# Embedding interactions on one core: ten one-hot tables instead of eight, groups of 256 samples, and the layers two groups later

## The chip, the cores and the metric

One Trainium2 core runs the whole program. The metric is device time in microseconds, the median of several timed executions of one kernel. One further execution is profiled, and all rows below come from it.

## The reference

2048 samples have 128 dense features and 26 ids, one for each table. A sample's 27 vectors of 128 numbers are its dense features and its 26 table rows. All 351 products of two of them go, with the dense features (twice), through three layers.

```python
e = jnp.stack([tbl_0[ids[:, 0]], ..., tbl_25[ids[:, 25]]], axis=1)
combined = jnp.concatenate([dense_features[:, None, :], e], axis=1)       # 2048 x 27 x 128
interactions = jnp.einsum('bnd,bmd->bnm', combined, combined)
z = jnp.concatenate([dense_features, interactions[:, _TRIU_I, _TRIU_J]], axis=1)
h = jnp.concatenate([z, r_dense_features], axis=1)                        # 607 columns
h = jnp.maximum(h @ W_top1 + b_top1, 0.0)                                 # 512
h = jnp.maximum(h @ W_top2 + b_top2, 0.0)                                 # 256
y = h @ W_top3
```

Twelve tables (8 to 11, 15 to 19, 23 to 25) have 1000 rows; the others have 1250 to 125000.

## The kernel before

**Two ways to a table row.** Eight 1000-row tables (`LOOKED`) are kept in SBUF, split into a high and a low part, whose products are added. A *look* (`look`, L333) multiplies them with a 0/1 matrix `match` that the vector engine makes by comparing the samples' ids with row numbers (`matches`, L465): 16 matmuls of 256 samples each, and the result already has features along the partitions. The other 18 tables are *gathered* (`gather_tile`, L294): GpSimd issues one indirect DMA for each table and tile of 128 samples, 288 in all, and TensorE transposes what lands (`turn`, L319), in groups of four tables.

**Stages of a tile.** `turned` holds the 27 vectors of each sample. `gram` (L354) multiplies them with themselves, 27x27, one small matmul a sample. The result is copied out (L451), written by SP to a DRAM scratch and read back along the diagonals (`repack`), so that `pairs` holds 3 chunks of 117 products by 128 samples. Then `layer1` (L365, L368), `layer2` (L379) and `layer3` (L386) run on 128 samples.

**Order.** All orders are written out by hand; the engines meet by semaphores. One iteration of the loop over `m` does two tiles, that is 256 samples: 8 looks, 9 groups of turns (36 transposes), 4 gram steps and two sets of layers. The layers stand one tile behind the grams. `rows` has two buffers of 18 tables, so a tile's first gather waits until the tile two before has been turned. There is one PSUM bank for looks; ACT copies six of the eight to `looked_sb` (L564) and puts all of them in place later (`unpack`, L576).

**Start.** SP loads the eight tables of 500 KB, 125 rows each, one after another (L255). ACT rounds each to its high part (L554), DVE takes the difference (L473). ACT does all eight before it copies the first look out (L564).

Of the kernel before, what the change touches and what calls it, by code (L numbers as in the profile page):

```python
# [9 lines left out]
SLOT = 28  # L30
LOOKED = [8, 9, 10, 11, 15, 16, 17, 18]
GATHERED = [k for k in range(TABLES) if k not in LOOKED]
LOOKS = len(LOOKED)
HALF = LOOKS // 2
EARLY = 2
STAGED = LOOKS - 2
PARTS = 8
GROUP_OF = 4
GROUPS = -(-len(GATHERED) // GROUP_OF)
STEPS = 2  # L40
AT_LAYER = [1, 2, 3]
IN_QUADRANT = P // STEPS // 4
SHIFTS = (FEATURES - 1) // 2
WRAPS = FEATURES - SHIFTS
CHUNK_I = 9
CHUNKS = FEATURES // CHUNK_I
CHUNK_ROWS = CHUNK_I * SHIFTS
BANK = 512
# [6 lines left out]
def tables_of(group):  # L55
    return GATHERED[group * GROUP_OF:(group + 1) * GROUP_OF]


def runs_of(some_tables):

    runs = []
    for n, k in enumerate(some_tables):
        if runs and runs[-1][1] + runs[-1][2] == k:
            runs[-1][2] += 1
        else:
            runs.append([n, k, 1])
    return runs


def looks_after(m, u, group):  # L70

    looks = [(m + 1, r) for r in range(HALF)] if u else [(m, r) for r in range(HALF, LOOKS)]
    if isinstance(m, int) and m + u == 0:
        looks = [(0, r) for r in range(EARLY, LOOKS)]
        return [look for n, look in enumerate(looks) if n * GROUPS // len(looks) == group]
    return [look for n, look in enumerate(looks) if n * (GROUPS - 1) // len(looks) == group]


def build(nc, dense_t, index_rows, look_ids_rows, tables, w1_dense, w1_pairs, b1, w2, b2, w3, y):
    fp32, fp32r, int32 = mybir.dt.float32, mybir.dt.float32r, mybir.dt.int32
# [3 lines left out]
    tiles = batch // P  # L86
    assert batch % (2 * P) == 0 and tiles >= 6
    look_rows = tables[LOOKED[0]].shape[0] // PARTS

    assert all(tables[k].shape[0] == look_rows * PARTS for k in LOOKED)  # L90
    assert look_rows <= P and look_rows * PARTS <= 4096 and 2 <= LOOKS <= 8 and LOOKS % 2 == 0
    assert FEATURES < 32 and batch <= FEATURES * P

    ctx = ExitStack()
    with ctx:
# [9 lines left out]

        rows = [sbuf(f"rows{u}", [P, len(GATHERED), D]) for u in range(2)]
        index = sbuf("index", [P, tiles, TABLES], int32)
        turned = sbuf("turned", [D, 2, P, SLOT])
        grams = [sbuf(f"grams{u}", [P, FEATURES, P]) for u in range(2)]
        pairs = [sbuf(f"pairs{u}", [P, CHUNKS, P]) for u in range(2)]  # L110
        hidden1 = sbuf("hidden1", [P, L1, P])
        hidden2 = sbuf("hidden2", [P, L2, P])
        y_row = grams[0][32:33].rearrange("p a b -> p (a b)")[:, 0:batch]
        dense_sb = sbuf("dense_sb", [D, batch])
        identity = sbuf("identity", [P, P])


        look_ids = sbuf("look_ids", [P, LOOKS, 2 * P], int32)
        row_number = sbuf("row_number", [P, PARTS], int32)
        table_high = sbuf("table_high", [P, LOOKS, PARTS, D], fp32r)  # L120
        table_low = sbuf("table_low", [P, LOOKS, PARTS, D], fp32r)
        looked_sb = sbuf("looked_sb", [D, STAGED, 2 * P])
        match = [sbuf(f"match{b}", [P, PARTS, 2 * P], fp32r) for b in range(2)]
        w1_dense_two = sbuf("w1_dense_two", [D, 2, H1])
        w1_dense_sum = w1_dense_two[:, 0, :]
        w1_pairs_sb = sbuf("w1_pairs_sb", [CHUNK_ROWS, CHUNKS, H1])
# [4 lines left out]

        scratch = [nc.dram_tensor(f"scratch{u}", (FEATURES, FEATURES + SHIFTS, P), fp32).ap() for u in range(2)]

        def raw_table(n):


            place = turned[0:look_rows, 1] if n < 2 else grams[(n - 2) // 3][0:look_rows]
            at = (n if n < 2 else (n - 2) % 3) * PARTS * D
            return place.rearrange("p a b -> p (a b)")[:, at:at + PARTS * D]

        turn_ps = [psum(f"turn_ps{b}", [P, BANK]) for b in range(2)]
        gram_ps = [psum(f"gram_ps{b}", [P, BANK]) for b in range(2)]
        layer1_ps = [psum(f"layer1_ps{h}", [P, L1 // 2, P]) for h in range(2)]
        layer2_ps = layer1_ps[0]
        layer3_ps = layer1_ps[1][0:1, 0, :]
        row_number_ps = psum("row_number_ps", [P, PARTS])
        look_ps = psum("look_ps", [P, BANK])

        index_in = sem("index_in")
        look_ids_in = [sem(f"look_ids_in{h}") for h in range(2)]
        raw_table_in = [sem(f"raw_table_in{n}") for n in range(LOOKS)]
        dense_in = sem("dense_in")
        weights_in = sem("weights_in")

        gathered = [[sem(f"gathered{u}_{g}") for g in range(GROUPS)] for u in range(2)]
        tiles_opened = sem("tiles_opened")
# [3 lines left out]
        row_numbers_copied = sem("row_numbers_copied")  # L162
        tables_high = sem("tables_high")
        tables_split = sem("tables_split")
        weights_summed = sem("weights_summed")
        turn_done = [sem(f"turn_done{u}") for u in range(2)]
        turned_dve = sem("turned_dve")
        turned_act = sem("turned_act")
# [3 lines left out]
        unpacked = sem("unpacked")  # L172
        gram_done = sem("gram_done")
        grams_dve = sem("grams_dve")
        grams_act = sem("grams_act")
        scratch_in = [sem(f"scratch_in{u}") for u in range(2)]
        wraps_in = [sem(f"wraps_in{u}") for u in range(2)]
        pairs_in = [sem(f"pairs_in{u}") for u in range(2)]
# [6 lines left out]
        y_stored = sem("y_stored")  # L185

        READS = CHUNKS * 16

        def after(eng, sem, count):

            if not isinstance(count, int) or count > 0:
                eng.wait_ge(sem, count)

        def bank_of(u, group):

            return (GROUPS * u + group) % 2

        def groups_in_bank(bank, m, u, group):

            return GROUPS * m + (GROUPS * u + group + 1 - bank) // 2  # L200

        def next_look(m, r):
            return (m, r + 1) if r + 1 < LOOKS else (m + 1, 0)

        def has_next(m, r):
            return not (isinstance(m, int) and (m, r) == (tiles // 2 - 1, LOOKS - 1))

        block = ctx.enter_context(nc.Block())

        @block.sync  # L210
        def _(sp):
            def known(value):

                return value if isinstance(value, int) else sp.snap(sp.to_reg(value))

            def load_look_ids(m, h):

                row, matched = (known(v) for v in (2 * m + h, LOOKS * (m - 1) + HALF * (h + 1)))

                after(sp, match_ready, matched)  # L220
                sp.dma_start(look_ids[:, HALF * h:HALF * (h + 1), :].rearrange("p n s -> p (n s)"),
                             look_ids_rows[bass.ds(row, 1)].broadcast_to([P, HALF * 2 * P])).then_inc(
                                 look_ids_in[h], 16)
# [56 lines left out]
            for u in range(2):  # L280
                repack(last_m, u)
# [381 lines left out]
```

## Time and profile before

| | us |
|---|---|
| median of 3 runs (411.86 to 413.2) | 412.48 |
| profiled execution | 414.85 |
| its span, from the first to the last instruction | 413.0 |
| busy: PE / GpSimd / DVE / ACT | 329.0 / 275.3 / 231.0 / 142.9 |
| mean granted TensorE clock, of full speed | 0.971 |

The busy time of GpSimd leaves out what it needs between two DMA issues, so it understates how full that engine is. Busy PE contains matmuls whose starts lie closer together than they are long: prices are read from start to start.

### The profile page before, as it was taken

To read this page: it belongs to the slowest core of one execution; us is meant where nothing else is said; L and a number is where in the kernel's file an instruction comes from. 1 tells how busy PE (TensorE), PEld (TensorE's weight loads), DVE (VectorE), ACT (ScalarE), POOL (GpSimd) and SP (SyncE) were. 2 spreads that over 40 slices of the span, in tenths; PEclk is the share of its full clock that TensorE was granted. 3 is DMA by queue.
4 is the path that set the end of the run, shared out by engine and by line. 5 is a ranking of instruction groups with operands and counts; after the bars stand their busy time and mean duration, and the time that the engine had idled before them with its cause. 6 is when DMAs were issued, how large, how long until landed. Compare 5 with 4: busy or idle time off the path is not lost.

```text
span 413.0 us, 14244 instructions
## 1 busy us (share of the span) xinstructions
PE 329.0 (80%) x6240; PEld 303.9 (74%) x6240; DVE 231.0 (56%) x234; ACT 142.9 (35%) x305; POOL 275.3 (67%) x295
## 2 busy tenths in 40 slices
PE   0300487999999999999989897989898895977676
PEld 0300486989898989897979796979888895966675
DVE  2244288686758676866666656576476656332211
ACT  1222216326333633363336231553236332442211
POOL 5777704777777777777777777777777777776000
PEclk9999998999999999999999998999999998998889
DMA  6444662254443434352424333342525142324020
GB/s 182 156 160 164 214 197 75 68 154 111 116 108 109 117 104 116 98 144 77 133 82 122 99 105 112 94 125 63 156 65 152 51 118 53 99 71 109 15 64 1
DMA packets 20763, 44.99 MB, mean 109 GB/s; under 512 B 6198, under 2 KB 11942, under 8 KB 20179
## 3 DMA queue, kind: packets, MB, share of 16 engines
q1 hardware_dynamic: 11524, 25.76, 20.3%
q0 software_dynamic: 9216, 18.89, 17.2%
q8 instruction: 18, 0.29, 0.3%
q14 instruction: 5, 0.04, 0.0%
HBM read 37.27 MB, written 7.36 MB: 108 GB/s over the span
## 4 chain that ended last, share of the span: by engine, by line
POOL 39%; PE 27%; issue 14%; DMA 7%; SPq 5%; ACT 4%; DVE 3%; POOLq 0%; ACTq 0%
POOL rows L294 39%; PE look_ps L333 11%; DMA grams<-in_table 6%; SPq L255 4%; PE gram_ps L354 4%; PE layer_ps L368 4%; PE layer_ps L379 3%; PE turn_ps L319 3%; ACT turned L576 2%; PE layer_ps L365 2%; DVE match L465 2%; DVE grams L451 1%; PE layer_ps L386 1%; DMA rows<-in_table,index 1%; ACT hidden L548 0%
## 5 line engine op out<-in xcount | busy, mean ns | idle before, releaser
L294 POOL DMA_INDIRECT rows<-in_table,index x288 | 274.5, 953 | 104.9 <-issue 86.5
L333 PE MATMUL look_ps<-match,table_high 125*128 125x256 f32 x512 | 137.9, 305 | 50.2 <-ACT looked_sb L564 27.7
L465 DVE TENSOR_TENSOR match<-look_ids,row_number_ps 125x2048 fp32r<-125x2048 int32 x64 | 145.8, 2280 | 6.5 <-DMA look_ids<-in_look_ids_rows 4.3
L333 PEld LDWEIGHTS look_ps<-match,table_high 125*128 125x128 f32 x512 | 103.2, 202 | 54.0 <-issue 52.4
L333 PE MATMUL look_ps<-match,table_low 125*128 125x256 f32 x512 | 132.2, 293 | 0.0
L333 PEld LDWEIGHTS look_ps<-match,table_low 125*128 125x128 f32 x512 | 103.8, 203 | 0.0
L451 DVE COPY grams<-gram_ps 27x432 f32<-27x432 f32 x64 | 38.2, 597 | 51.3 <-PE gram_ps L354 50.8
L319 PE MATMUL turn_ps<-identity,rows 128*128 128x128 f32 x288 | 47.2, 287 | 21.4 <-DMA rows<-in_table,index 21.3
L354 PE MATMUL gram_ps<-turned 128*27 128x27 f32 x4096 | 54.0, 194 | 5.1 <-issue 1.9
L354 PEld LDWEIGHTS gram_ps<-turned 128*27 128x27 f32 x4096 | 44.8, 105 | 15.4 <-issue 8.7
L368 PE MATMUL layer_ps<-pairs,w_pairs_sb 117*128 117x128 f32 x384 | 55.4, 282 | 0.0
L319 PEld LDWEIGHTS turn_ps<-identity,rows 128*128 128x128 f32 x288 | 33.0, 144 | 27.3 <-issue 21.1
L451 ACT COPY grams<-gram_ps 27x432 f32<-27x432 f32 x64 | 32.8, 512 | 58.1 <-PE gram_ps L354 57.7
L438 DVE COPY turned<-turn_ps 128x512 f32<-128x512 f32 (+3 forms) x48 | 27.8, 594 | 42.1 <-PE turn_ps L319 41.4
L368 PEld LDWEIGHTS layer_ps<-pairs,w_pairs_sb 117*128 117x128 f32 x384 | 50.1, 199 | 0.0
L564 ACT COPY looked_sb<-look_ps 128x256 f32<-128x256 f32 x48 | 17.9, 372 | 92.7 <-PE look_ps L333 92.7
L481 DVE TENSOR_SCALAR hidden<-layer_ps,b_sb 128x128 f32<-128x128 f32 x32 | 9.8, 347 | 44.6 <-PE layer_ps L379 42.5
L548 ACT ACTIVATE hidden<-layer_ps,b_sb 128x128 f32<-128x128 f32 x64 | 20.0, 364 | 42.0 <-PE layer_ps L368 42.0
L379 PE MATMUL layer_ps<-hidden,w_sb 128*128 128x128 f32 x256 | 32.9, 284 | 1.4 <-ACT hidden L548 1.4
L438 ACT COPY turned<-turn_ps 128x512 f32<-128x512 f32 (+3 forms) x48 | 27.1, 584 | 19.5 <-PE turn_ps L319 19.3
L379 PEld LDWEIGHTS layer_ps<-hidden,w_sb 128*128 128x128 f32 x256 | 31.6, 201 | 1.8 <-ACT hidden L548 1.8
L365 PE MATMUL layer_ps<-dense_sb,w_dense_two 128*128 (+1 forms) x128 | 27.3, 295 | 2.3 <-DVE grams L488 1.8
(21 smaller groups left out, 101.8 us busy)
## 6 DMA issues: line engine op xcount, KB each, us to landing
look_ids<-in_look_ids_rows SPq DMA_DIRECT2D x16, 512.0 KB, 4.2
scratch<-grams SPq DMA_DIRECT2D x16, 364.5 KB
rows<-in_table,index POOLq DMA_INDIRECT x288
grams<-in_table SPq DMA_DIRECT2D x6, 500.0 KB
pairs<-scratch SPq DMA_DIRECT2D x48, 58.5 KB
scratch<-grams SPq DMA_DIRECT2D x16, 84.5 KB
dense_sb<-in_dense_t SPq DMA_DIRECT2D x1, 1024.0 KB, 5.0
turned<-in_table SPq DMA_DIRECT2D x2, 500.0 KB
```

Source lines behind the costliest of these rows:

```text
L294: pool.indirect_dma_start(out=rows[u][:, group * GROUP_OF + n, :], out_offset=None, in_=tables[k], in_offset=bass.IndirectOffsetOnAxis(ap= ...
L319: last = nc.tensor.transpose(turn_ps[bank][:, n * P:(n + 1) * P], rows[u][:, group * GROUP_OF + n, :], identity[:])
L333: last = nc.tensor.matmul(look_ps[:, 0:2 * P], part[0:look_rows, r, c, :], match[r % 2][0:look_rows, c, :], start=(c == 0 and part is tabl ...
L354: last = nc.tensor.matmul(gram_ps[step][s * 32:s * 32 + FEATURES, x * FEATURES:(x + 1) * FEATURES], of_sample, of_sample, start=True, stop ...
L365: nc.tensor.matmul(layer1_ps[o // 2][:, o % 2, :], w1_dense_sum[:, o * P:(o + 1) * P], dense_sb[:, bass.ts(2 * m + u, P)], start=True, sto ...
L368: last = nc.tensor.matmul(layer1_ps[o // 2][:, o % 2, :], w1_pairs_sb[:, c, o * P:(o + 1) * P], pairs[u][0:CHUNK_ROWS, c, :], start=False, ...
L379: last = nc.tensor.matmul(layer2_ps[:, o, :], w2_sb[:, c, o * P:(o + 1) * P], hidden1[:, c, :], start=(c == 0), stop=(c == L1 - 1))
L438: last = copy(turned[:, u, :, 1 + k:1 + k + length], bank[:, n * P:(n + length) * P].rearrange("d (f s) -> d s f", f=length))
L451: last = copy(grams[u][0:FEATURES, :, sample:sample + IN_QUADRANT], gram_ps[step][s * 32:s * 32 + FEATURES, 0:IN_QUADRANT * FEATURES].rear ...
L465: nc.vector.tensor_tensor(match[r % 2][0:look_rows], look_ids[0:look_rows, r].unsqueeze(1).broadcast_to(shape), row_number_ps[0:look_rows] ...
L548: last = nc.scalar.activation(hidden1[:, o, :], layer1_ps[o // 2][:, o % 2, :], ACT.Relu, bias=b1_sb[:, o:o + 1])
L564: nc.scalar.copy(looked_sb[:, r, :], look_ps[:, 0:2 * P]).then_inc(looked, 1)
```

## The change

- **Tables.** Ten tables are looked up, 16 gathered. The tenth looked table (23) is gathered for groups 0 to 3 (`EXTRA`, two more indirect DMAs and one more turn for each of these groups) and looked up from group 4 on.
- **Groups.** Everything works on groups of 256 samples: a group has 10 looks (9 in groups 0 to 3), 8 turns of four tables, 4 gram steps of 64 samples, one set of layers of 256 columns. Weights of the gram matmuls are 32 columns wide (five are not used).
- **Looks ahead.** Six looks of the next group are made while this group's last gathers land. PSUM has two banks for looks of two each, three for turns and grams (`mid_ps`), two for layers. ACT does every copy out of PSUM, DVE only matches and splits. `unpack` is gone: looks go straight to `turned`, of which there are two.
- **Layers.** The layers of group g-2 stand among the grams of g-1 and the turns of g.
- **Start.** Tables go through three raw buffers, each loaded as 112 and 13 rows; splits and looks of groups 0 and 1 are interleaved table by table.
- **Repack.** `grams` has 128 partitions; the scratch gets 864 and 416 KB a group, the read back is 12 DMAs of 117 rows of 256 bytes (before: 3 of 117 rows of 512 bytes a tile). In the last group the three chunks are issued by SP, ACT and GpSimd. `rows` is freed four tables at a time.
- The scratch that holds the software DMA's descriptors is set to 4096 bytes; ids for the looks are int16.

```diff
-LOOKED = [8, 9, 10, 11, 15, 16, 17, 18]
+LOOKED = [8, 9, 10, 11, 15, 16, 17, 18, 19, 23]
...
+EXTRA = (0, 1, 2, 3)
...
+N = 256
...
+        def load_pairs(eng, g, c, signal):
+            for s in range(QUADS):
...
+                eng.dma_start(pairs[0:CHUNK_ROWS, g % 2, c, s * IN_QUAD:(s + 1) * IN_QUAD], skewed).then_inc(signal, 16)
...
+            def load_raw(r):
...
+                after(sp, tables_split, r - RAWS + 1)
+                sp.dma_start(raw[b][0:SPREAD], rows_of[0:SPREAD]).then_inc(raw_in[b], 16)
+                sp.dma_start(raw[b][SPREAD:table_rows], rows_of[SPREAD:table_rows]).then_inc(raw_in[b], 16)
...
+            def repack(g):
+                sp.wait_ge(mid_out, gram_number(g, STEPS - 1) + 1)
...
+                sp.dma_start(flat[:, 0:FEATURES], grams[:]).then_inc(scratch_in, 16)
+                sp.dma_start(flat[:, FEATURES:WIDTH], grams[:, 0:SHIFTS]).then_inc(scratch_in, 16)
+                sp.wait_ge(scratch_in, SCRATCH_DMAS * (g + 1))
...
+                for c in range(CHUNKS if g + 1 < groups else 1):
+                    load_pairs(sp, g, c, pairs_in)
```

TensorE's new loop (the whole of it; `range` of g is 1 to 6):

```diff
+            for g in range(1, groups - 1):
...
+                gram(g - 1, 0)
+                turn(g, 0)
+                look(g, 6)
+                if g >= 2:
+                    layer1(g - 2, 0)
+                    layer1(g - 2, 1)
+                gram(g - 1, 1)
+                turn(g, 1)
+                look(g, 7)
+                if g >= 2:
+                    layer1(g - 2, 2)
+                    layer1(g - 2, 3)
+                gram(g - 1, 2)
+                turn(g, 2)
+                look(g, 8)
+                if g >= 2:
+                    layer2(g - 2)
+                gram(g - 1, 3)
+                turn(g, 3)
+                if g in EXTRA:
+                    turn_extra(g)
+                else:
+                    look(g, 9)
+                if g >= 2:
+                    layer3(g - 2)
+                turn(g, 4)
+                look(g + 1, 0)
+                look(g + 1, 1)
+                turn(g, 5)
+                look(g + 1, 2)
+                turn(g, 6)
+                look(g + 1, 3)
+                turn(g, 7)
+                look(g + 1, 4)
+                look(g + 1, 5)
```

**GpSimd's gathers.** The queue from its first gather on, before (288 gathers, a wait for each 18):

```order
L303 IOTA row_number 128x8
L294 DMA rows<-in_table,index 128x128 [waits index_in]
L294 DMA rows<-in_table,index 128x128 x35
L294 DMA rows<-in_table,index 128x128 [waits turn_done0]
L294 DMA rows<-in_table,index 128x128 x17
```

and after the change (`extra` is the tenth table's buffer; `turn_done` frees four tables of `rows`):

```order
L311 AFFINE_SELECT identity<-identity 128x128 [waits zeroed]
L322 DMA rows<-in_table,index 128x128 [waits first_index_in]
L322 DMA rows<-in_table,index 128x128 x15
L333 DMA extra<-in_table,index 128x128 [waits index_in]
L333 DMA extra<-in_table,index 128x128
L322 DMA rows<-in_table,index 128x128 [waits index_in]
L322 DMA rows<-in_table,index 128x128 x15
L322 DMA rows<-in_table,index 128x128 [waits turn_done]
L322 DMA rows<-in_table,index 128x128 x3
```

The queue is 264 gathers long instead of 288, and the waits stand before each four gathers; the two of `extra` come behind the first tile of groups 0 to 3.

**ACT's start.** Its queue from the last three of the eight table splits (`table_high`) on, before:

```order
L554 CAST table_high<-grams 125x1024 [waits raw_table_in5]
L554 CAST table_high<-grams 125x1024 [waits raw_table_in6]
L554 CAST table_high<-grams 125x1024 [waits raw_table_in7]
L564 COPY looked_sb<-look_ps 128x256 [waits look_done] x2
L564 COPY looked_sb<-look_ps 128x256 [waits look_done,tables_split,dense_in]
L564 COPY looked_sb<-look_ps 128x256 [waits look_done]
L438 COPY turned<-turn_ps 128x128x4 [waits turn_done0]
L564 COPY looked_sb<-look_ps 128x256 [waits look_done] x2
```

and after, from the first split on:

```order
L554 CAST table_high<-grams 125x1024 [waits raw_in0]
L554 CAST table_high<-pairs 125x1024 [waits raw_in1]
L554 CAST table_high<-hidden 125x1024 [waits raw_in2]
L554 CAST table_high<-grams 125x1024 [waits raw_in0]
L561 COPY turned<-look_ps 128x256x2 [waits look_done] x2
L554 CAST table_high<-pairs 125x1024 [waits raw_in1]
L572 COPY turned<-mid_ps 128x128x4 [waits turn_done]
L554 CAST table_high<-hidden 125x1024 [waits raw_in2]
L572 COPY turned<-mid_ps 128x128x4 [waits turn_done]
L561 COPY turned<-look_ps 128x256x2 [waits look_done] x2
```

The first copy of a look stood behind eight splits and stands behind four; the others alternate with splits and turns.

**TensorE's end.** Behind the last turns, before (the grams are those of the last tile):

```order
L354 MATMUL gram_ps<-turned 27x27 [waits looked,grams_dve,unpacked,grams_act,turned_act,turned_dve]
L354 MATMUL gram_ps<-turned 27x27 x63
L354 MATMUL gram_ps<-turned 27x27 [waits grams_act,grams_dve]
L354 MATMUL gram_ps<-turned 27x27 x63
L386 MATMUL layer_ps<-hidden,w_sb 1x128 [waits hidden2_ready]
L386 MATMUL layer_ps<-hidden,w_sb 1x128
L365 MATMUL layer_ps<-dense_sb,w_dense_two 128x128 [waits y_copied,pairs_in0]
L368 MATMUL layer_ps<-pairs,w_pairs_sb 128x128 x3
```

and after, from the last turn on:

```order
L364 MATMUL mid_ps<-identity,rows 128x128 [waits gathered1_3,mid_out]
L364 MATMUL mid_ps<-identity,rows 128x128 x3
L405 MATMUL layer_ps<-dense,w_dense_sum 128x256
L408 MATMUL layer_ps<-pairs,w_pairs_sb 128x256 x3
L390 MATMUL mid_ps<-turned 32x27 [waits mid_out]
L390 MATMUL mid_ps<-turned 32x27 x63
L417 MATMUL layer_ps<-hidden,w_sb 128x256 [waits hidden1_ready]
L417 MATMUL layer_ps<-hidden,w_sb 128x256 x7
L390 MATMUL mid_ps<-turned 32x27 [waits mid_out]
L390 MATMUL mid_ps<-turned 32x27 x63
L424 MATMUL layer_ps<-hidden,w_sb 1x256 [waits hidden2_ready]
L424 MATMUL layer_ps<-hidden,w_sb 1x256
```

Before, one layer 2, two gram steps and a layer 3 stood between the last turn and the last two layer sets (128 samples each); now a quarter of a layer 1, two gram steps, a layer 2 and a layer 3 of 256 samples stand there, and two layer sets of 256 samples follow.

## Rows read from the trace of the kernel before

**Rows 1.** The head of the page.

```profile
span 413.0 us, 14244 instructions
```

**Rows 2.** Windows: length, busy us (instructions) of each engine, clock, DMA share, GB/s.

```profile
103.76:143.74 39.98, 39.15 (x780) 36.40 (x781) 27.57 (x29) 16.67 (x38) 30.23 (x33) 1.00 0.41 113
...
166.52:380.00 213.48, 190.61 (x3809) 175.88 (x3806) 125.38 (x132) 81.55 (x181) 161.37 (x171) 0.97 0.36 100
```

**Rows 3.** Timeline of GpSimd: start, us, instruction [idle before, releaser].

```profile
4.22 1.10 POOL L294 DMA_INDIRECT rows<-in_table,index  x1 [2.65 <-DMA index<-in_index_rows]
...
66.66 0.94 POOL L294 DMA_INDIRECT rows<-in_table,index  x1 [15.08 <-PE turn_ps L319]
...
126.58 0.94 POOL L294 DMA_INDIRECT rows<-in_table,index  x1 [0.30 <-PE turn_ps L319]
```

**Rows 4.** The chain that ended last, at the last gather: start, us, what.

```profile
380.00 2.79 DMA rows<-in_table,index
```

**Rows 5.** Timeline of TensorE: the first matmul of the first two looks.

```profile
15.93 0.55 PE L333 MATMUL look_ps<-match,table_high 125*128 125x256 f32 x1 [15.93 <-DVE table_low L473]
...
47.42 0.56 PE L333 MATMUL look_ps<-match,table_high 125*128 125x256 f32 x1 [27.74 <-ACT looked_sb L564]
```

**Rows 6.** Timeline of ACT: the first look is copied out.

```profile
46.91 0.36 ACT L564 COPY looked_sb<-look_ps 128x256 f32<-128x256 f32 x1
```

**Rows 7.** Timeline of DVE: the first match.

```profile
6.04 2.29 DVE L465 TENSOR_TENSOR match<-look_ids,row_number_ps 125x2048 fp32r<-125x2048 int32 x1 [4.26 <-DMA look_ids<-in_look_ids_rows]
```

**Rows 8.** Groups by line: count, busy us, mean ns, idle before.

```profile
L465 DVE TENSOR_TENSOR match<-look_ids,row_number_ps 125x2048 fp32r<-125x2048 int32 x64 | 145.8, 2280 | 6.5 <-DMA look_ids<-in_look_ids_rows 4.3 <-PE look_ps L333 1.7
...
L354 PEld LDWEIGHTS gram_ps<-turned 128*27 128x27 f32 x4096 | 44.8, 105 | 15.4 <-issue 8.7 <-DVE turned L438 0.3
...
L438 ACT COPY turned<-turn_ps 128x512 f32<-128x512 f32 x24 | 17.6, 733 | 12.8 <-PE turn_ps L319 12.6
...
L473 DVE TENSOR_TENSOR table_low<-grams,table_high 125x1024 fp32r<-125x1024 f32 x6 | 7.4, 1226 | 15.5 <-ACT table_high L554 15.5
```

**Rows 9.** Timeline of TensorE around 200 to 221 us.

```profile
199.70 0.60 PE L319 MATMUL turn_ps<-identity,rows 128*128 128x128 f32 x4
200.06 0.36 PE L333 MATMUL look_ps<-match,table_high 125*128 125x256 f32 x1
...
202.06 1.95 PE L379 MATMUL layer_ps<-hidden,w_sb 128*128 128x128 f32 x16
203.85 0.60 PE L319 MATMUL turn_ps<-identity,rows 128*128 128x128 f32 x4
...
211.37 1.81 PE L354 MATMUL gram_ps<-turned 128*27 128x27 f32 x128
213.11 0.66 PE L319 MATMUL turn_ps<-identity,rows 128*128 128x128 f32 x4
...
217.52 0.48 PE L365 MATMUL layer_ps<-dense_sb,w_dense_two 128*128 x2
...
221.19 0.60 PE L319 MATMUL turn_ps<-identity,rows 128*128 128x128 f32 x4
```

**Rows 10.** Timeline of all engines at the end of the span.

```profile
383.32 3.43 PE L379 MATMUL layer_ps<-hidden,w_sb 128*128 128x128 f32 x16
...
392.57 0.28 SPq L234 DMA_DIRECT2D scratch<-grams  x1
...
396.44 2.34 SPq L249 DMA_DIRECT2D pairs<-scratch  x3
...
399.15 2.05 PE L379 MATMUL layer_ps<-hidden,w_sb 128*128 128x128 f32 x16 [0.71 <-ACT hidden L548]
...
401.90 0.60 PE L386 MATMUL layer_ps<-hidden,w_sb 128*1 128x128 f32 x4 [0.70 <-DVE hidden L481]
...
411.19 0.24 SPq L283 DMA_DIRECT2D out_y<-grams  x1
```

**Rows 11.** DMA issues: KB each, median us to landing.

```profile
dense_sb<-in_dense_t SPq DMA_DIRECT2D x1, 1024.0 KB, 5.0
```

More of the change, by code:

```diff
@@ L52, with build @@
 L2 = H2 // P
[L55 to L82, printed above, removed]
+def build(nc, dense_t, index_t, look_rows_t, tables, w1_dense, w1_pairs, b1, w2, b2, w3, y):
+    fp32, fp32r, int32, int16 = mybir.dt.float32, mybir.dt.float32r, mybir.dt.int32, mybir.dt.int16
     ALU = mybir.AluOpType
@@ L198, in groups_in_bank, with looks_of, look_order @@
[L198 to L206, printed above, removed]
-        block = ctx.enter_context(nc.Block())
+        def looks_of(g):
+            return LOOKS - 1 if g in EXTRA else LOOKS
+        def look_order():
+            yield from ((g, r) for r in range(AHEAD) for g in (0, 1))
+            yield from ((g, r) for g in (0, 1) for r in range(AHEAD, looks_of(g)))
+            yield from ((g, r) for g in range(2, groups) for r in range(looks_of(g)))
@@ L310, in _ @@
+            pool.wait_ge(scratch_in, SCRATCH_DMAS * groups)
+            pool.wait_ge(layer1_done, 2 * (groups - 2))
+            load_pairs(pool, groups - 1, CHUNKS - 1, last_chunk_in)
         @block.tensor
         def _(pe):
[L312 to L321 removed]
@@ L388, in layer3 @@
                 last.then_inc(layer3_done, 1)
-            def tile(m, u, grams=True, layers=True, looks=True, last=False):
-                gm = m - 1 + u
-                for group in range(GROUPS):
-                    turn(m, u, group)
-                    if looks:
-                        for look_of in looks_after(m, u, group):
-                            look(*look_of)
-                    if grams and group < STEPS:
-                        gram(gm, 1 - u, group)
-                    if layers and group == AT_LAYER[0]:
-                        layer1(m - 1, u)
-                    if layers and group == AT_LAYER[1] and not last:
-                        layer2(m - 1, u)
-                    if layers and group == AT_LAYER[2] and not last:
-                        layer3(m - 1, u)
@@ new lines, in _ @@
+            g = groups - 1
+            for k in range(STEPS):
+                gram(g - 1, k)
+                turn(g, k)
+                look(g, AHEAD + k)
+            layer1(g - 2, 0)
+            layer1(g - 2, 1)
+            gram(g, 0)
+            layer1(g - 2, 2)
+            gram(g, 1)
+            turn(g, 4)
+            turn(g, 5)
+            turn(g, 6)
+            turn(g, 7)
+            layer1(g - 2, 3)
+            gram(g, 2)
+            layer2(g - 2)
+            gram(g, 3)
+            layer3(g - 2)
```

801 lines of the change are left out of this document (451 added, 350 removed).

## The prediction, made blind

> **What bounds the kernel now.** I read the windows first: they show two regimes. In one whole iteration, from 103.76 to 143.74 us, TensorE is busy 39.15 of 39.98 us at clock 1.00; from 166.52 to 380.00 us it is busy 190.6 of 213.5 us [rows 2]. GpSimd's busy time hides that it is the full engine there: in its timeline the gathers stand 0.30 us apart, 0.94 us each; the first starts at 4.22 us, and one waited for long, 15.08 us, for a turn [rows 3]. The last, the 288th, starts at 380.00 us [rows 4]. So a gather takes (380.00 - 4.22 - 15.08) / 287 = 1.257 us, and an iteration's 36 take 45.2 us, against TensorE's 39.98 us. The chain that ended last passes through that last gather, which has landed 2.79 us after its start, at 382.79 us; the end is 413.0 us [rows 1], a tail of 30.2 us.
>
> The start decides where GpSimd first waits. TensorE's first look is at 15.93 us, its second at 47.42 us [rows 5], because ACT copies the first one out only at 46.91 us, behind its eighth split [rows 6]. Till then the `rows` buffers fill, and GpSimd stands.
>
> So the time is: 4.22 us, 288 gathers, the 15.08 us stall, and the tail.
>
> **GpSimd's term.** 16 x 16 + 4 x 2 = 264 gathers, 24 fewer. The wait before each four instead of before each eighteen adds nothing: a gather whose wait for a turn is fulfilled starts after the same 0.30 us as any other, as at 126.58 us [rows 3]. The stall goes if four rows are turned in time. The last gather then starts at 4.22 + 263 x 1.257 = 334.8 us and has landed at 337.6 us, 45.2 us earlier. By the same grid the last gathers of groups 1, 2, 3 and 4 (the 68th, 102nd, 136th and 168th) have landed at 91.2, 134.0, 176.7 and 216.9 us.
>
> **The start.** For each of the first six tables DVE makes two matches of 2.28 us and a split of 1.23 us [rows 8], 5.8 us; for each of the next three 3.5 us. From about 6 us, where its first match is now [rows 7], that ends at 6 + 34.8 + 10.5 = 51 us. Loading a table has to keep this pace: dense features of 1024 KB land in 5.0 us [rows 11], and 500 KB cannot be slower than DVE's 5.8 us unless they come as before, in about 4.5 us ((47.42 - 15.93) / 7), which would do too. I take 56 us for the end of the start, with a few us of half clock. Turns 0 to 4 stand among these looks, so the first `rows` buffer is free well before GpSimd comes to it again at 4.2 + 34 x 1.257 = 47 us.
>
> In group 1, which has no layers, TensorE has work for 28 us (4 x 1.74 + 8.5 x 0.36 + 9 x 2.00, by the prices below) and then waits for the gathers: its last turn stands at 91.2 us. Behind it stand two looks. So a start that ends anywhere before about 65 us costs nothing.
>
> **TensorE's term.** From start to start: a turn 0.36, a look 2.00, a layer 2 of 128 columns 1.79, a gram step 1.74, a layer 1 of 128 columns 3.67 us [rows 9]; a layer 3 0.60 us [rows 10]. Eight looks, nine turns, four grams and two layer sets add to 38.3 us; the iteration took 39.98 us, so 1.7 us go into handing over. I start from the 39.98 us:
> - two looks more, +4.0 us (one look and half a turn more in groups 2 and 3, +2.2 us); one turn fewer, -0.36 us.
> - Layers of 256 columns are not in the trace. Above, they cost as much as two of 128 columns. Below, each of a matmul's two passes costs what a look's single pass over 256 columns costs (2.00 / 16 = 0.125 us), which would halve a layer set. I take the upper end: same number type, same columns, so 12.1 us a group and no change.
> - Gram weights of 32 columns instead of 27: the same 1.74 us below, 32/27 of it (2.06 us) above. I take the lower end, since what streams is still 27 columns.
> - Copies out, matches: ACT's copy of a turn is 0.73 us, DVE's match 2.28 us [rows 8], so ten matches are 23 us of a group and lie beside TensorE. Work queued behind a late copy is TensorE's third next step, since three banks rotate.
>
> So a group takes 41.8 us (2 and 3) and 43.6 us (4 to 6) on TensorE, against GpSimd's 42.7 and 40.2 us. Group 2 starts at 91.2 + 0.4 + 4.0 = 95.6 us. Group 2 is done at 138.4 us (134.0 and what stands behind its last turn), group 3 at 181.1 us (176.7 + 4.4), group 4 at 181.1 + 43.6 = 224.7, group 5 at 268.3, group 6 at 311.9 us: from group 4 on TensorE is the slower of the two, slightly. Group 7 up to its second four turns has 4 x (1.74 + 0.36 + 2.00), three quarters of a layer 1 (5.5) and two grams (3.5), 25.4 us: 337.3 us. The last gather has landed at 337.6 us. The two meet; the turns are done at 338.8 us.
>
> **The tail.** A quarter of a layer 1 (1.84), gram (1.74), layer 2 (3.58), gram (1.74), layer 3 (1.2), to 348.9 us. Layer 1 of group 6 (7.34), 1.0 us for its last two activations (0.71 us for two of half the size [rows 10]), layer 2 (3.58), 0.95, layer 3 (1.2): 363.0 us. The same again for group 7: 377.0 us. Copy and store: 0.4, then 1.8 us as now (411.19 us to the end [rows 1, 10]). Span 379.2 us.
>
> Beside it runs group 7's repack. From the last gram's copy (348.3 us) the scratch write of 1280 KB lies between the 3.9 us of today's 449 KB (392.57 to 396.44 us [rows 10]) and that times 2.85, 11 us; nearest is the load of 1024 KB in 5.0 us [rows 11], so 6.2 us. Twelve read backs at 0.78 us [rows 10], split over three queues, land by about 362 us, 1 us before layer 1 wants them. With 11 us it is 3 us late, and the end with it.
>
> **Sum.** 413.0 - 45.2 (24 gathers and the stall) + 1.2 (turns end behind the landing) + 10.2 (tail 40.4 instead of 30.2) = 379.2 us. The profiled execution lies 1.85 us above its span and 2.37 us above the median, so the median should be 378.7 us.
>
> **Weighing a rule against the trace.** The trace's read backs are of 512-byte rows, and an issue of 117 rows takes 0.78 us [rows 10]; the change makes them 256 bytes. The Trainium skill, DMA: Bandwidth & Descriptors, Specifications, names 512 B as the least transfer for line rate and says that below it the engine reads, modifies and writes. By that rule the read backs could take twice as long; the rival "repack" below says what this would do. No row here has 256-byte reads.
>
> **Rivals.**
> - *TensorE sets the pace.* If gram weights cost their columns (+1.3 us a group) and waits of 1 us a group come in, groups 2 to 7 take 8 to 14 us more and the median is 387 to 393 us. For it: TensorE has no slack from group 4 on. Against: unpacking and the single look bank are gone, and some of the 1.7 us with them. The page TensorE: Matmul & The Clock Gate of the Trainium skill, section LDWEIGHTS, lets load time grow with columns; the mean weight load is 0.105 us for 27 columns [rows 8].
> - *The start stays long.* If loads and DVE's waits for looks stretch it to 80 us, group 1 ends near 107 us instead of 95.6 us and group 3 at 107 + 2 x 41.8 = 190.6 us instead of 181.1 us: the median is 388 us.
> - *Repack sets the pace (the other side).* A group's fourth gram ends 25 us into the period, and layer 1 wants its pairs 4 us into the next: 22.7 us for copy (0.55), scratch (6.2), 12 issues (9.4) and landing (2), 18 us. If issues double (18.7) and the scratch takes 11 us, it is 32 us; some five groups then wait 9.6 us each: 427 us. It is slower than before from about 30 us on. For it: the smaller rows. Against: 18 us leave a margin of 4 us.
> - *The change does not do what it says*, TensorE being late by half clock or waits in every group: 405 to 415 us.
>
> If TensorE hands over faster than I think, GpSimd sets the end of the turns (338.0 us). TensorE then idles before it and starts the tail at half clock, as at 383.32 us, where a layer 2 took 3.43 us instead of 1.95 [rows 9, 10]: 2 to 3 us given back, the same time.
>
> **How the numbers follow.** My forecast, 372 to 387 us: 0.62. TensorE's pace, 387 to 400 us: 0.15. A long start, 384 to 393 us: 0.12. Repack: 0.08, half of it slower than before. No change: 0.03. The range 370 to 396 us holds the first and most of the next two, 0.85. About 0.3% is what a measurement of this kernel can tell. Faster by more: 0.62 + 0.15 + 0.12 + 0.04 + 0.01 = 0.94; within: 0.02; slower: 0.04.
>
> **What would show it.** Right: gathers on a 1.25 us grid without a stall from 4 to 335 us; TensorE's groups 4 to 6 at 42 to 44 us; first gram near 56 us; the tail near 40 us, its last layer 1 not waiting for `pairs`. Wrong: GpSimd waiting for turns; TensorE waiting for `pairs` in layer 1; a gram step above 1.9 us; layer sets far from 12 us; half clock inside the groups.

## The result and the profile after

The changed kernel takes 385.16 us (median of 4 runs, 383.7 to 386.47), the kernel before 412.84 us beside it (4 runs, 411.86 to 415.06): a ratio of 0.932, 95% interval 0.926 to 0.938. It is faster by 27.7 us where 34 were forecast; the time lies in the range given. The profiled execution took 386.31 us.

The page of the kernel after: its span, then busy time by engine, the instruction queue, and the chain's shares.

```profile
span 384.3 us, 13008 instructions
...
PE 339.5 (88%) x5992; PEld 301.9 (79%) x5992; DVE 184.1 (48%) x90; ACT 126.0 (33%) x215; POOL 258.0 (67%) x275
...
q8 instruction: 47, 0.77, 0.8%
...
PE 66%; POOL 18%; issue 7%; DMA 5%; DVE 2%; ACT 1%; ACTq 0%; DVEq 0%
```

The same row of the page before:

```profile
POOL 39%; PE 27%; issue 14%; DMA 7%; SPq 5%; ACT 4%; DVE 3%; POOLq 0%; ACTq 0%
```

GpSimd had 39% of the chain and TensorE 27%; now TensorE has two thirds. Its stages, as windows (columns as in [rows 2]): group 1, groups 2 to 6, group 7 up to the end of its turns, and the tail.

```profile
58.64:103.90 45.26, 33.58 (x693) 31.12 (x694) 18.65 (x10) 11.25 (x18) 34.29 (x37) 0.89 0.61 175
103.90:144.70 40.80, 40.01 (x743) 35.81 (x743) 20.73 (x10) 14.18 (x26) 30.74 (x34) 1.00 0.35 97
144.70:186.56 41.86, 40.35 (x750) 36.04 (x752) 20.13 (x10) 14.30 (x26) 31.80 (x34) 1.00 0.40 112
186.56:229.30 42.74, 41.99 (x766) 37.57 (x768) 23.06 (x11) 14.36 (x25) 32.13 (x35) 1.00 0.41 113
229.30:271.66 42.36, 41.65 (x763) 37.35 (x767) 22.69 (x11) 14.27 (x25) 32.09 (x34) 1.00 0.38 108
271.66:314.35 42.69, 41.88 (x763) 37.47 (x767) 22.69 (x11) 14.30 (x25) 32.16 (x35) 1.00 0.39 110
314.35:346.30 31.95, 29.44 (x889) 26.19 (x890) 6.90 (x4) 10.69 (x19) 19.76 (x21) 0.95 0.34 100
346.30:384.30 38.00, 32.33 (x388) 25.02 (x387) 0.00 (x0) 9.72 (x23) 2.49 (x4) 1.00 0.14 48
```

From 103.90 us on TensorE is busy nearly throughout, at a granted clock of 1.00 but for group 7 (0.95); group 1 is where it waits (33.58 of 45.26 us busy). GpSimd, in its timeline (the answer to [rows 3]):

```profile
5.28 1.17 POOL L322 DMA_INDIRECT rows<-in_table,index  x1 [3.72 <-DMA index<-in_index]
...
23.01 1.63 POOL L322 DMA_INDIRECT rows<-in_table,index  x1 [0.30 <-issue]
...
75.74 0.94 POOL L322 DMA_INDIRECT rows<-in_table,index  x1 [0.30 <-PE mid_ps L364]
...
339.27 0.94 POOL L322 DMA_INDIRECT rows<-in_table,index  x1 [0.30 <-issue]
```

No gather stands longer than 0.31 us behind the one before it: the stall of 15.08 us is gone. Seven gathers that start from 23.01 to 52.43 us take 1.63 to 1.79 us. The last starts 40.7 us earlier than before, and the end is 45.0 us behind it, where it was 33.0.

The chain that ended last, at the ends of groups 1 and 3 and in group 7 (start, us, what):

```profile
94.48 3.44 DMA rows<-in_table,index
98.06 1.09 PE mid_ps L364 x4
99.15 4.80 PE look_ps L352 x32
...
179.39 2.58 DMA rows<-in_table,index
182.73 3.84 PE look_ps L352 x32
...
324.94 1.57 issue
326.51 0.80 PE mid_ps L364 x3
327.31 3.12 PE look_ps L352 x16
330.43 1.43 PE mid_ps L390 x84
332.73 1.92 PE look_ps L352 x16
```

Groups 1 and 3 end with a gather's landing, a turn and two looks: 6.0 us from landing to end in group 1 (97.92 to 103.9 us), 4.6 us in group 3. The two looks take 4.80 and 3.84 us; the granted clock of group 1's window is 0.89 and TensorE had just stood for 3.00 us. In group 7 nothing that the profile shows holds TensorE for 1.57 us in the middle of a turn; the look after it takes 3.12 us, the next one 1.92.

The tail, in the timeline of SP's DMA queue and of TensorE:

```profile
354.68 0.33 SPq L240 DMA_DIRECT2D scratch<-grams  x1
...
361.02 3.13 SPq L215 DMA_DIRECT2D pairs<-scratch  x4
...
362.95 3.72 PE L417 MATMUL layer_ps<-hidden,w_sb 128*128 128x256 f32 x16 [0.93 <-ACT hidden L592]
...
368.55 0.70 PE L405 MATMUL layer_ps<-dense,w_dense_sum 128*128 128x256 f32 x2
369.09 1.46 PE L408 MATMUL layer_ps<-pairs,w_pairs_sb 117*128 117x256 f32 x6
```

The scratch write keeps the read backs waiting for 6.3 us, and the last layer 1 follows without a wait for `pairs`.

### The profile page after: what moved, and what is told of

The parts are those of the page before. It is cut to its first block, busy times and chain, and to the rows that moved or that the text cites. A ratio compares the mean times of both kernels' runs of the same rounds, so it can differ in the third digit from the quotient of the medians.

```text
span 384.3 us, 13008 instructions
## 1 busy us (share of the span) xinstructions
PE 339.5 (88%) x5992; PEld 301.9 (79%) x5992; DVE 184.1 (48%) x90; ACT 126.0 (33%) x215; POOL 258.0 (67%) x275
## 4 chain that ended last, share of the span: by engine, by line
PE 66%; POOL 18%; issue 7%; DMA 5%; DVE 2%; ACT 1%; ACTq 0%; DVEq 0%
PE look_ps L352 24%; POOL rows L322 17%; PE mid_ps L390 12%; PE layer_ps L408 11%; PE layer_ps L417 7%; PE mid_ps L364 7%; PE layer_ps L405 4%; DMA rows<-in_table,index 4%; DVE match L519 2%; PE layer_ps L424 2%; DMA index<-in_index 1%; POOL extra L333 0%; ACT hidden L598 0%; ACT hidden L592 0%; ACTq L215 0%
## 5 line engine op out<-in xcount | busy, mean ns | idle before, releaser
L322 POOL DMA_INDIRECT rows<-in_table,index x256 | 247.2, 966 | 81.4 <-issue 76.8
L519 DVE TENSOR_TENSOR match<-look_ids,row_number_ps 125x2048 fp32r<-125x2048 int16 x76 | 172.6, 2285 | 136.7 <-PE look_ps L352 129.7
L390 PEld LDWEIGHTS mid_ps<-turned 128*32 128x32 f32 x4096 | 45.7, 109 | 19.0 <-issue 15.0
L390 PE MATMUL mid_ps<-turned 128*32 128x27 f32 x4096 | 54.7, 195 | 5.5 <-ACT turned L576 2.1
L561 ACT COPY turned<-look_ps 128x512 f32<-128x512 f32 (+1 forms) x40 | 31.7, 792 | 70.6 <-PE look_ps L352 67.4
L364 PE MATMUL mid_ps<-identity,rows 128*128 128x128 f32 x256 | 41.5, 287 | 13.9 <-DMA rows<-in_table,index 11.6
L572 ACT COPY turned<-mid_ps 128x512 f32<-128x512 f32 x64 | 42.5, 671 | 24.3 <-PE mid_ps L364 24.1
L408 PE MATMUL layer_ps<-pairs,w_pairs_sb 117*128 117x256 f32 x192 | 46.7, 379 | 0.0
L364 PEld LDWEIGHTS mid_ps<-identity,rows 128*128 128x128 f32 x256 | 29.1, 144 | 18.4 <-issue 14.8
L417 PE MATMUL layer_ps<-hidden,w_sb 128*128 128x256 f32 x128 | 29.2, 382 | 1.9 <-ACT hidden L592 1.9
```

The lines of the kernel that those rows point to most:

```text
L322: pool.indirect_dma_start(out=rows[j % 2][:, at, :], out_offset=None, in_=tables[GATHERED[at]], in_offset=bass.IndirectOffsetOnAxis(ap=ind ...
L364: last = nc.tensor.transpose(mid_ps[number % 3][:, n * P:(n + 1) * P], rows[j % 2][:, u * UNIT_OF + n, :], identity[:])
L390: last = nc.tensor.matmul(mid_ps[number % 3][s * ROW:(s + 1) * ROW, i * FEATURES:(i + 1) * FEATURES], turned[g % 2][:, n:n + ROW], turned[ ...
L408: last = nc.tensor.matmul(layer_ps[o // 2][:, o % 2, :], w1_pairs_sb[0:CHUNK_ROWS, c, o * P:(o + 1) * P], pairs[0:CHUNK_ROWS, g % 2, c, :] ...
L417: last = nc.tensor.matmul(layer_ps[0][:, o, :], w2_sb[:, c, o * P:(o + 1) * P], hidden1[:, c, :], start=(c == 0), stop=(c == L1 - 1))
L519: nc.vector.tensor_tensor(match[number % 2][0:table_rows], look_ids[b][0:table_rows, r % 2].unsqueeze(1).broadcast_to(shape), row_number_p ...
```

## The experiments

"The change" below is the changed kernel, 385.16 us, span 384.3 us. Each experiment ran beside the kernel before (median 413.0 to 414.3 us).

### Which engine sets the pace: how often the tenth table is gathered

Three kernels move work between GpSimd and TensorE and leave the rest. More gathers, fewer looks:

```diff
-EXTRA = (0, 1, 2, 3)
+EXTRA = (0, 1, 2, 3, 4, 5, 6)
```

> The tenth looked table is gathered in groups 0 to 6 instead of 0 to 3: 270 gathers (+6, 7.5 us of GpSimd) and three looks fewer (-6 us of TensorE). Theory (GpSimd paces TensorE up to group 3, TensorE is the slower from group 4 on): group 6 ends near 314 us as now, since GpSimd's 42.5 us a group takes the place of TensorE's 42.6 us; the last gather lands near 349.5 us and the turns end 3 to 4 us later than now: 388 to 390 us against 385.2 us. Rival 'the length of GpSimd's queue sets the time': +7.5 us, 392.7 us. Rival 'TensorE's work sets the time': -6 us, 379 us.

390.6 us (390.3 to 392.13), ratio 0.945 (0.940 to 0.949); span 388.4 us. Its last gather starts at 347.07 us. The time lies 0.6 us above the 388 to 390 us of the theory, 2.1 us below the first rival and far from the second.

Fewer gathers, two more looks at the start (and one more split behind them):

```diff
-EXTRA = (0, 1, 2, 3)
+EXTRA = (2, 3)
...
-            turn_extra(0)
...
+            look(0, 9)
```

> The tenth table is gathered in groups 2 and 3 only: four gathers fewer, all ahead of group 2, and two looks more, in groups 0 and 1. Theory: TensorE has 11 us without work in group 1, so the two looks cost nothing, the last gather of group 1 lands 5 us earlier, groups 2 to 7 all start 5 us earlier: 379 to 381 us against 385.2 us. Rival 'TensorE's work sets the time': +4 us, 389 us.

381.78 us (6 runs, 380.94 to 382.91), ratio 0.923 (0.919 to 0.926); span 379.1 us, 0.8 us above what the theory gave. And none at all, `EXTRA = ()`:

> The tenth table is never gathered: 256 gathers (-8, 10 us of GpSimd), four looks more (+8 us of TensorE, two of them in groups 0 and 1). Theory: group 2 starts 5 us earlier, but TensorE then needs 42.7 us for each of groups 2 to 6 instead of 40.8 and 41.9 us in groups 2 and 3: about -2 us, 382 to 384 us. Rival 'the length of GpSimd's queue': -10 us, 375 us. Rival 'TensorE's work': +8 us, 393 us.

382.75 us (381.94 to 383.73), ratio 0.924 (0.919 to 0.928); span 381.8 us, although its last gather starts at 330.10 us, 9.2 us before the change's.

What TensorE's turns wait for in the view of waits (us in total, times, longest), first the change, then with seven groups gathered, then with two:

```profile
PE mid_ps L364 <- DMA rows<-in_table,index: 11.6, 5, 3.5
```

```profile
PE mid_ps L364 <- DMA rows<-in_table,index: 17.2, 8, 4.7
```

```profile
PE mid_ps L363 <- DMA rows<-in_table,index: 0.7, 1, 0.7
```

With two extra groups the wait for gathers is all but gone and 3.4 us come back; with none GpSimd has more slack and the time does not fall further. The page of that last kernel and its chain in group 1 say what holds it:

```profile
PE 81%; DVE 11%; issue 5%; DMA 1%; ACT 1%; SPq 0%; ACTq 0%; DVEq 0%
```

```profile
68.64 3.31 issue
...
75.63 3.80 issue
```

GpSimd is no longer on its chain, and in group 1 TensorE stands twice, 3.31 and 3.80 us, while nothing that the profile shows holds it (the same kind of gap as in group 7, below; the kernel with two extra groups has 1.85 and 3.47 us there). So in the change GpSimd sets the ends of groups 1 and 3, TensorE everything behind, and the extra gathers in groups 0 and 1 were too many. The kernel with `EXTRA = (2, 3)` has the lowest median of all that were run; from the one with none it can't be told apart (the intervals of the ratios overlap nearly whole).

### The start alone, in the kernel before

How much of the gain is the start? The kernel before, its splits and looks interleaved table by table, all else as it was:

```diff
-            for n in range(LOOKS):
-                split_high(n)
-            for r in range(EARLY):
-                take_look(0, r)
+            for n in range(3):
+                split_high(n)
+                if n > 0:
+                    take_look(0, n - 1)
...
                         for look_of in looks_after(m, u, group):
+                            if isinstance(m, int) and m + u == 0 and look_of[1] + 1 < LOOKS:
+                                split_high(look_of[1] + 1)
                             take_look(*look_of)
```

> The kernel before, with its start alone changed: ACT and DVE split table r, then serve the look of table r-1, instead of splitting all eight first. Gathers, looks, layers and their order on TensorE are as before. Theory: the first tile is turned by about 50 us, GpSimd's 15.1 us stall goes, and the time falls by 13 to 15 us to 398 to 400 us, since GpSimd's 45.2 us an iteration bound the rest. Rival: the stall comes back later or TensorE cannot follow, and less than 5 us are won (408 us or more).

417.47 us (414.82 to 419.61), ratio 1.010 (1.005 to 1.016): a miss. ACT's waits say why:

```profile
ACT table_high L553 <- DMA dense_sb<-in_dense_t: 25.7, 1, 25.7
```

ACT waits 25.7 us for the dense features, which stand behind all tables in the DMA queue, before it may copy the looks that free the bank. The order of the copies was changed but not what they stood behind, and GpSimd's stall stayed at 15.05 us. With that wait moved to the code that needs it:

```diff
-            act.wait_ge(dense_in, 16)
-            act.wait_ge(tables_split, 2)
...
+                if isinstance(m, int) and m == 0:
+                    act.wait_ge(dense_in, 16)
+                    act.wait_ge(tables_split, 2)
```

> The kernel before with its start alone changed, as in the run before, and ACT's wait for the dense features put off to where they are first used (in that run this wait, behind all tables on the DMA queue, had kept ACT and with it the looks standing until 51 us). Theory: the first tile is turned by about 50 us, GpSimd's 15.1 us stall goes, 398 to 400 us against 412.8 us. Rival: TensorE cannot follow or the stall comes back, 408 us or more.

402.59 us (401.97 to 404.48), ratio 0.976 (0.973 to 0.980); span 400.0 us. That is 2.6 us above the range of the theory, and well below its rival. GpSimd's timeline has no stall left (the longest waits for a turn are like this one), and the last gather starts at 367.04 us, 13.0 us earlier than before:

```profile
96.15 0.94 POOL L294 DMA_INDIRECT rows<-in_table,index  x1 [0.31 <-PE turn_ps L319]
```

So the start is worth 13.0 us between the two profiled spans (413.0 and 400.0 us), and 10.4 us between the medians (412.96 and 402.59 us): the profiled execution of before was 2.4 us above its median. The remaining 15.7 us of span (400.0 to 384.3) are the last gather's 367.04 to 339.27, 27.8 us earlier, less an end that is 12.0 us longer behind it (45.0 us, and 33.0 here).

### One load per table

```diff
-                sp.dma_start(raw[b][0:SPREAD], rows_of[0:SPREAD]).then_inc(raw_in[b], 16)
-                sp.dma_start(raw[b][SPREAD:table_rows], rows_of[SPREAD:table_rows]).then_inc(raw_in[b], 16)
+                sp.dma_start(raw[b], rows_of).then_inc(raw_in[b], 16)
```

> The changed kernel with each table loaded as one DMA of 125 rows, as before the change, instead of 112 and 13 rows. Theory (DVE's matches and splits pace the start at 5.8 us a table, and TensorE has 11 us to spare in group 1): a load of 4.4 us hides, no change but for the first table, 385 to 387 us. Rival 'the split load makes the start': 10 tables x 2 us later, the first gram near 75 us, 390 us or more.

384.8 us (384.19 to 385.74), ratio 0.931 (0.929 to 0.933): no change. ACT's wait for the tables that come into `grams` grows from 9.8 us in all (three waits) to 17.6 us (four), those for the other two buffers likewise. Not all of it hides behind DVE's matches, as the theory had it: the first gram starts at 63.47 us instead of 58.64. It costs nothing all the same, since group 1 has slack (the prediction let a start of up to about 65 us go free), and group 2 starts at 103.86 us, as in the change. The last gather of group 1 starts 2.3 us later (96.80 us), but lands after 2.53 us instead of 3.44, and the two looks behind it take 3.83 us instead of 4.80, at a granted clock of 1.00.

### Why seven gathers are slow

Each of the seven starts 0.25 to 0.41 us after a split on DVE, whose two operands both lie in SBUF, and none beside a match, whose row numbers lie in PSUM. Two splits and the gathers beside them in the change:

```profile
16.77 0.94 POOL L322 DMA_INDIRECT rows<-in_table,index  x1 [0.30 <-issue]
16.84 1.22 DVE L527 TENSOR_TENSOR table_low<-pairs,table_high 125x1024 fp32r<-125x1024 f32 x1
...
22.60 1.22 DVE L527 TENSOR_TENSOR table_low<-hidden,table_high 125x1024 fp32r<-125x1024 f32 x1
23.01 1.63 POOL L322 DMA_INDIRECT rows<-in_table,index  x1 [0.30 <-issue]
```

A gather that starts under a split ends 0.81 to 0.82 us after it; one that had started just before the split takes its 0.94 us. The match, made to read the same numbers from SBUF:

```diff
-row_number_ps[0:table_rows].unsqueeze(2).broadcast_to(shape)
+row_number[0:table_rows].unsqueeze(2).broadcast_to(shape)
```

> The changed kernel, DVE's matches reading the row numbers from SBUF instead of PSUM; nothing else. In the changed kernel 7 of the gathers under a table split (both operands in SBUF) take 1.63 to 1.79 us instead of 0.94. Theory 'a DVE operation with both operands in SBUF holds GpSimd's gather': each of the 76 matches (2.29 us) now lengthens a gather by 0.7 to 2 us, the mean gather rises from 0.97 us to 1.2 us or more, and the time by 30 us or more. Rival 'table loads on the DMA rings slow those gathers': the gathers and the time stay as they are, 385 us.

483.35 us (one run), span 481.4 us. The timeline of DVE and GpSimd:

```profile
100.84 2.29 DVE L519 TENSOR_TENSOR match<-look_ids,row_number 125x2048 fp32r<-125x2048 int16 x1 [3.11 <-PE look_ps L352]
101.35 2.60 POOL L322 DMA_INDIRECT rows<-in_table,index  x1 [0.30 <-issue]
104.26 0.94 POOL L322 DMA_INDIRECT rows<-in_table,index  x1 [0.30 <-issue]
```

The match takes its 2.29 us as before; the gather that starts under it takes 2.60 us and ends 0.82 us after it, the next takes 0.94. The mean gather rises from 966 to 1346 ns, which over 256 gathers is 97 us, the whole of the longer span (481.4 against 384.3 us). So an operation of DVE that reads two operands from SBUF holds a GpSimd gather that starts under it till it is done, and the splits do the same in the change.

### The last group's read backs on one queue

```diff
-                for c in range(CHUNKS if g + 1 < groups else 1):
+                for c in range(CHUNKS):
```

(and ACT's and GpSimd's two chunks removed, with their waits.)

> The changed kernel with all twelve read backs of the last group issued by SP instead of by SP, ACT and GpSimd. Theory: from 361 us on the twelve issues take 9.4 us and land near 372.5 us; layer 1 of the last group started at 368.6 us, so the end comes 3 to 4 us later, 388 to 389 us. Rival: the read backs were not what layer 1 waited next for, no change.

390.15 us (388.37 to 390.99), ratio 0.945 (0.943 to 0.948); the profiled execution took 388.37 us, its span 386.6 us. SP's queue and TensorE's wait:

```profile
359.48 9.38 SPq L215 DMA_DIRECT2D pairs<-scratch  x12
```

```profile
PE layer_ps L398 <- DMA pairs<-scratch: 2.2, 1, 2.2
```

Twelve issues on one queue take 9.38 us, and layer 1 waits 2.2 us, the 2.3 us of span. The median lies 5.0 us above the change's, and the rest of that is not in the one trace. So the split over three queues pays, by 2.3 us of span and 5.0 us between the medians. In the change ACT's fourth issue starts at 365.1 us and a read back lands 2.1 to 2.3 us after its start, so the pairs are there some 1.2 us before layer 1 starts at 368.55 us: a margin as thin as the predicted 1 us.

### The gap in group 7

TensorE stops for 1.57 us behind the first transpose of a turn that has four and no wait between them. Two kernels above whose TensorE does the same up to there, the one with one load per table and the one with all read backs on SP, have it at the same transpose (1.62 and 1.03 us); so it belongs to a place in the program. There only gram, turn and look follow each other, some 300 instructions in 4.2 us, since a gram step alone is 128 weight loads and 128 matmuls. Instructions come in 47 packets of 0.77 MB in all, 16 KB each; in 0.2 us slices of the DMA view they stand 3.6 to 4.8 us apart there (320.0, 323.6, 327.6, 332.4 us). The kernel before, with loops, had 18 packets. Three kernels test whether it is their arrival. A quarter of a layer 1 is moved between the grams:

```diff
                 look(g, AHEAD + k)
-            layer1(g - 2, 0)
+                if k == 1:
+                    layer1(g - 2, 0)
             layer1(g - 2, 1)
```

> A quarter of group 5's layer 1 (1.84 us of TensorE work, 16 instructions) is moved from behind group 7's fourth look to behind its second. Theory (instructions arrive too slowly where gram, turn and look follow each other with nothing else between): the gap of 1.0 to 1.6 us in the middle of the third turn of that stretch goes, or falls under 0.5 us, and TensorE's clock stays 1.00 in the stretch; 382.5 to 384.5 us instead of 385.2. Rival (the third turn waits for something of its own): the gap stays at 1.0 us or more in the same turn; 385 us. Both: the quarter that is gone from before the first gram of group 7 no longer covers ACT's copies there, which can cost up to 1 us.

384.0 us (383.45 to 384.27), ratio 0.927 (0.923 to 0.930), span 382.3 us. The gap is gone there; 0.18 us remain up to 331.44 and 0.53 us up to 341.11 us, and the clock from 314 to 346 us is 1.00 instead of 0.95. The span is 2.0 us shorter; the intervals of the ratios overlap, so the time alone doesn't settle it.

The same in the kernel with `EXTRA = (2, 3)`:

> The version with the tenth table gathered in groups 2 and 3 alone (381.8 us), with the same quarter of layer 1 moved. Theory: its gap of 0.67 us just ahead of that turn goes too, 380.5 to 381.8 us. Rival: no change, 381.8 us, or up to 1 us more where the quarter no longer covers ACT's copies.

382.25 us (381.38 to 383.15), ratio 0.923 (0.919 to 0.927): no gain, and its gap stays, 0.56 us instead of 0.67. A miss for the remedy.

And the change with 16 matmuls made twice in group 0:

```diff
-                for c in range(PARTS):
+                for c in (*range(PARTS if (g, r) == (0, 8) else 0), *range(PARTS)):
```

> Look 8 of group 0 is computed twice over (its first 16 matmuls are made again and overwritten), 32 more TensorE instructions at about 58 us, where TensorE later waits for the gathers. Theory (instruction delivery in pieces of 16 KB): the gap of group 7 is tied to a place counted in instructions, so it stands 16 matmuls earlier in the program, among the last 15 or so of the gram ahead of the turn. Rival (tied to the turn): it stays behind the turn's first transpose. Time: within 1.5 us of 385 us by both.

385.05 us (one run), span 383.1 us. TensorE's timeline:

```profile
323.75 1.71 PE L390 MATMUL mid_ps<-turned 128*32 128x27 f32 x114
325.89 0.32 PE L390 MATMUL mid_ps<-turned 128*32 128x27 f32 x14 [0.43 <-issue]
326.14 0.66 PE L364 MATMUL mid_ps<-identity,rows 128*128 128x128 f32 x4
```

The turn is whole, and the gap stands 14 matmuls ahead of it: 15 matmuls earlier than in the change, for 16 added. The same trace has a second such place, in group 1, of which the kernel with one load per table (first row) has the unpadded form:

```profile
86.34 0.33 PE L363 MATMUL mid_ps<-identity,rows 128*128 128x128 f32 x1 [1.84 <-issue]
```

```profile
81.83 0.32 PE L390 MATMUL mid_ps<-turned 128*32 128x27 f32 x13 [0.89 <-issue]
```

Without the padding the gap stands ahead of a turn's fourth transpose, with it 13 matmuls ahead of that turn: 16 matmuls earlier, and in both behind 849 matmuls from the start of the program. So the gap counts instructions, it doesn't belong to the turn. In six kernels TensorE resumes 2.3 to 2.9 us after an instruction packet begins (packets are read in slices of 0.2 us: packet 323.6, resumed 326.51 in the change; 325.2 and 328.13; 324.0 and 326.61; 314.6 and 317.17; 316.2 and 318.78; 323.4 and 325.89). That its cause is late instructions fits all of this but is not shown directly: the profile has no row for TensorE waiting for them. The change's second gap, which ends at 340.36 us, doesn't fit the 2.3 to 2.9 us (packets begin at 332.4 and 340.0 us), and why a gap is 0.4 us in one kernel and 1.6 in another stays open.

## Why the prediction was right, and where its sizes were off

**The bound, and what the change does to it: right.** 288 gathers on GpSimd set the end of before; without the stall and with 24 gathers fewer the last gather starts 40.7 us earlier (45.2 forecast), and TensorE takes over from group 4 on, as the prediction said. The kernels with more and with fewer extra gathers confirm both sides.

**The sum, by its own terms.** 379.2 forecast, 384.3 us measured:

| Term | forecast | measured | difference |
|---|---|---|---|
| group 2 starts | 95.6 | 103.9 | +8.3 |
| group 2 | 42.8 | 40.8 | -2.0 |
| group 3 | 42.7 | 41.86 | -0.8 |
| groups 4 to 6 | 130.8 | 127.8 | -3.0 |
| group 7 to its last turn | 26.9 | 31.95 | +5.0 |
| tail | 40.4 | 38.0 | -2.4 |

The errors go both ways: 13.3 us too little in two terms, 8.2 us too much in the others. That the sum is off by only 5.1 us is in part luck.

- **GpSimd's term was mis-sized, and this is the largest error (6.7 of the 8.3 us by which group 2 starts late).** "Landed at 91.2" for group 1's last gather was 97.92 us. The first gather starts 1.06 us later (its index comes by ACT's queue); its step of 1.257 us was an average over the whole kernel, while the undisturbed step is 1.249 (from 94.48 to 339.27 us, 196 steps) and seven gathers in the start take 0.7 to 0.85 us more; landing took 3.44 us for 2.79. The start of before had such gathers too, inside the average. Behind the landing came 6.0 us for the forecast 4.4: TensorE had stood for 3.00 us, and the two looks took 4.80 us, where 3.84 us is the price in group 3 at clock 1.00 (group 1 as a whole was granted 0.89). Half clock inside a group was named as a sign of being wrong, but not priced there.
- **The start: right.** First gram at 58.64 us (56 forecast), and slack in group 1: TensorE is busy 33.58 of 45.26 us. The rival "long start" (80 us) didn't happen; group 2's late start has another cause, above.
- **TensorE's term: the mechanism right, the layers priced high.** A gram of 32 columns takes 1.75 us (314.28 to 316.03 us), the lower end, though its mean weight load rose from 0.105 to 0.109 us. A layer 1 of 256 columns takes 6.9 us (four quarters of 1.73 us), a layer 2 3.46, a layer 3 0.95: a layer set 11.3 us where 12.1 was taken, still near the upper bound. Groups 4 to 6 take 42.4 to 42.7 us, inside the 42 to 44 us named; the rival "TensorE sets the pace" with 387 us is not met, since the gram does not get longer with its weights' columns.
- **Group 7: missed.** The gap (1.57 us), the slow look behind it (3.12 us for 1.92; the group was granted 0.95 of the clock) and a second gap of 0.43 us that ends at 340.36 us make up 3.2 of the 5.0 us. Nothing in the prediction looked at the supply of instructions, though straight-line code for 8 groups stood in the change.
- **The tail: right.** 38.0 us; the scratch write took 6.3 us for 6.2, and the pairs came some 1.2 us before layer 1. The forecast's "about 362 us" for them does not follow from its own terms, which give 359.6 us (348.3 + 6.2 + 4 x 0.78 + 2): a margin of 3.4 us. Much of it went because ACT issues its first read back 1.1 us behind SP (362.12 against 361.02 us) and its four issues take 3.8 us instead of 3.1. That the margin came out near the stated 1 us is luck.
- **Repack, the rival on the other side: refuted.** No layer 1 waits for pairs. The rule that was weighed beside it (the Trainium skill, DMA: Bandwidth & Descriptors, Specifications: at least 512 B for line rate) shows no cost in issue: twelve issues of 256-byte rows take 9.38 us, 0.78 each, as an issue of 512-byte rows did [rows 10], and a read back lands 2.1 to 2.3 us after its start, about the 2 us forecast.

## What to carry to other kernels

An average step hides disturbances that are all in one place: take the step of an undisturbed stretch and count the disturbed instructions apart, above all where the change makes that stretch the one that decides. When a change hands the bound from one engine to another, try the number that shares the work between them on both sides; here two extra groups beat four, and none at all was no better than two. An order that is changed in one queue gains nothing while the same queue still waits for something that comes late: one misplaced wait for the dense features lay between 417.47 and 402.59 us.

## What the hardware showed that was not expected

- **A DVE operation with two SBUF operands holds a GpSimd gather.** 1.63 to 1.79 us instead of 0.94 beside a split of 1.22 us; 2.60 us beside a match of 2.29 us, and still 0.94 beside a match that reads one operand from PSUM. The Trainium skill, SBUF — State Buffer, Who interferes with whom, says that an operation of DVE with two inputs in SBUF contends with a GpSimd instruction that reads SBUF. The traces agree for the issue of an indirect DMA whose offsets lie in SBUF; only gathers that start under the operation are held, till 0.82 us after its end.
- **Straight-line code may keep TensorE waiting for its instructions (argued, not shown).** The program came in 47 packets of 16 KB, and gaps in which TensorE waits for nothing that the profile shows stand in or close behind gram steps: 0.43 to 1.62 us in group 7, and in the kernel with no extra gathers 3.31 and 3.80 us in group 1. The Trainium skill, Advanced Engine Details and Errata, ISA Cache, gives lines of 16 KB or 256 instructions. The packets' size agrees, and so does their number: TensorE's 5992 matmuls and as many weight loads would fill 46.8 of them.
